# A mixture-of-experts layer behind two attentions: fewer expert tiles in two stages, rows fetched by token number and outputs written to token rows

## The reference

```
x = x + cross_attention(layernorm(x), ctx)       # 64 queries on 1601 keys, softmax
x = x + pairwise_attention(layernorm(x))         # relu(signed_sqrt(q_i + k_j)) for all pairs i, j of 64
x = x + experts(layernorm(x)):
    scores = sigmoid(xf @ gate.T)                # 8 experts, in 4 groups of 2; groups by scores + bias
    2 best groups, in them the 2 best experts; weights = their scores over their sum
    for e in range(8):                           # I = 256
        y += w[:, e] * ((silu(xf @ gate_proj[e].T) * (xf @ up_proj[e].T)) @ down_proj[e].T)
```

## Time and the profile before

| | |
|---|---|
| median of 3 runs | 634.35 us (634.19 to 635.99) |
| the profiled execution | 636.18 us, span 634.4 us, mean granted clock 0.954 |
| PE busy | 554.6 us (87%) |
| DVE busy | 421.3 us (66%) |
| ACT busy | 265.2 us (42%) |
| DMA | 196.3 MB, 309 GB/s over the span |

### The profile page before, as it was taken

One profiled execution on the slowest core, in us unless ns is written; L12 is line 12 of the kernel. 1 busy time (PEld: TensorE's weight loads), 2 busy tenths in 40 slices (PEclk: granted clock), 3 DMA queues, 4 the chain that ended last, 5 costly groups with the idle time before them and its releaser, 6 DMA issues.

```text
span 634.4 us, 7981 instructions
## 1 busy us (share of the span) xinstructions
PE 554.6 (87%) x2608; PEld 313.6 (49%) x2608; DVE 421.3 (66%) x721; ACT 265.2 (42%) x380; POOL 61.3 (10%) x76
## 2 busy tenths in 40 slices
PE   7899388999999999999999996669898989888960
PEld 3586133534445344453563442445666756655740
DVE  3775112568788687886978887785986865676623
ACT  0340021352623526235254182429666546465720
POOL 4000100100001000010000013000000610410004
PEclk9999777999999999999999999888999999999995
DMA  9999629979799797997959988634867899999916
GB/s 309 359 403 407 262 91 371 381 258 385 279 369 397 264 386 268 365 400 265 386 201 310 389 313 308 254 122 155 299 250 258 285 376 397 398 395 419 375 67 198
DMA packets 91677, 196.30 MB, mean 309 GB/s; under 512 B 5872, under 2 KB 39152, under 8 KB 87808
## 3 DMA queue, kind: packets, MB, share of 16 engines
q1 hardware_dynamic: 82400, 177.29, 75.9%
q10 hardware_dynamic: 6688, 10.25, 4.4%
q0 software_dynamic: 2560, 8.39, 3.7%
HBM read 173.89 MB, written 22.02 MB: 309 GB/s over the span
## 4 chain that ended last, share of the span: by engine, by line
PE 56%; DMA 15%; DVE 15%; ACT 5%; issue 4%; POOL 2%; SPq 2%; POOLq 0%; DVEq 0%; ACTq 0%
PE ps L1401 13%; PE ps L1491 11%; DMA gu_raw<-in_gu_t 6%; PE ps L1648 4%; DMA keys<-in_ctx_t 3%; DVE plane L925 2%; DVE wgu_lo L1167 2%; DMA rows<-in_x 2%; PE ps L1555 2%; PE ps L1618 2%; PE ps L1619 2%; DMA vals<-in_ctx 2%; PE ps L1626 2%; PE ps L314 2%; PE ps L315 2%
## 5 line engine op out<-in xcount | busy, mean ns | idle before, releaser
L1491 PE MATMUL ps<-vals,probs_t 128*64 128x512 f32 (+1 forms) x416 | 99.1, 616 | 2.2 <-DMA vals<-in_ctx 2.2
L1401 PE MATMUL ps<-keys,q_cur 128*64 128x401 f32 (+1 forms) x512 | 91.3, 509 | 8.6 <-DMA keys<-in_ctx_t 8.6
L1167 DVE TENSOR_TENSOR wgu_lo<-gu_raw,wgu_hi 128x2048 fp32r<-128x2048 f32 x30 | 68.6, 2288 | 37.8 <-ACT wgu_hi L688 37.8
L688 ACT CAST wgu_hi<-gu_raw 128x2048 fp32r<-128x2048 f32 x30 | 57.0, 1900 | 24.2 <-DMA gu_raw<-in_gu_t 24.2
L1401 PEld LDWEIGHTS ps<-keys,q_cur 128*64 128x64 f32 x512 | 35.5, 138 | 58.3 <-issue 49.0
L1648 PE MATMUL ps<-dn_raw,ht 128*128 128x512 f32 x120 | 58.4, 610 | 1.4 <-ACT ht L710 1.4
L1491 PEld LDWEIGHTS ps<-vals,probs_t 128*64 128x64 f32 (+1 forms) x416 | 28.1, 140 | 58.0 <-issue 57.7
L1618 PE MATMUL ps<-wgu_hi,xt_hi 128*128 128x512 f32 x120 | 50.8, 423 | 3.6 <-DVE xt_lo L1156 3.6
L1619 PE MATMUL ps<-wgu_hi,xt_lo 128*128 128x512 f32 x120 | 48.7, 406 | 0.0
L1005 DVE SCALAR_TENSOR_TENSOR plane<-plane,ps 128x512 f32<-128x512 f32 x64 | 40.3, 681 | 3.4 <-PE ps L1555 3.3
L517 POOL TENSOR_TENSOR x_in<-x_in,bv_b 128x512 f32<-128x512 f32 x8 | 10.1, 1267 | 276.8 <-DMA x_in<-in_x 276.8
(11 more groups left out here) (207 smaller groups left out, 939.7 us busy)
## 6 DMA issues: line engine op xcount, KB each, us to landing
keys<-in_ctx_t SPq DMA_DIRECT2D x24, 1604.0 KB, 12.9
gu_raw<-in_gu_t SPq DMA_DIRECT2D x30, 1024.0 KB, 7.5
vals<-in_ctx SPq DMA_DIRECT2D x32, 768.0 KB, 12.1
vals<-in_ctx SPq DMA_DIRECT2D x16, 1024.0 KB, 9.7
dn_raw<-in_down_t SPq DMA_DIRECT2D x30, 512.0 KB, 6.8
keys<-in_ctx_t SPq DMA_DIRECT2D x8, 1592.0 KB, 16.9
vals<-in_ctx SPq DMA_DIRECT2D x16, 512.0 KB
xs<-vy ACTq DMA_DIRECT2D x2, 3840.0 KB, 32.4
```

Of the source, the lines that this page charges most:

```text
L688: act.copy(wgu_hi[i % 2][:], gu_raw[i % 3][:]).then_inc(gu_hi_ok, 1)
L1167: dve.tensor_tensor(wgu_lo[i % 2][:], gu_raw[i % 3][:], wgu_hi[i % 2][:].bitcast(F32), ALU.subtract).then_inc(gu_lo_ok, 1)
L1401: ins = pe.matmul(ps[b * SQ:(b + 1) * SQ, c, 0:width(c)], q_cur[:, k, b * SQ:(b + 1) * SQ], keys[:, c, b * KD + k, 0:width(c)], start=(k = ...
L1491: ins = pe.matmul(ps[b * SQ:(b + 1) * SQ, OUT, :], probs_t[0:w, n, b * SQ:(b + 1) * SQ], vals[0:w, n % RING, b, :], start=(n == 0), stop=( ...
```

## The change

- One plan of 23 tiles (2*8+7). After token tiles 0 to 5 (`NA = 6`) only 5 tiles leave in the first stage, `FULL = 2*6-7`: those many are full whatever the data, since 1536 rows over 8 experts have at least 5 full tiles. Rows that are left over are placed again with those of token tiles 6 and 7, in the other 18. These start only when pair 7 has been gated and placed.
- The zeroing, `xs` and its scatters are gone. Normalised rows are stored in token order (`n3d`, direct DMAs). For each tile, the token number in each place is found by a product on PE of one-hot matrices (place within the tile by token) with a grid (token by tile, holding the token's number): `ids(g)`, `take_ids(g)`. POOL's `gather(i)` then fetches a tile's rows by number, and POOL's `scatter(i)` writes a tile's output straight to the token's row of `ys` (first or second choice); empty places write to spare rows behind them.
- So the final fetch is by direct DMAs: `load_first` (2 of 1 MB) when tile 21 is stored, `load_second` (8 of 256 KB) after the last.
- The 5 tiles of stage 1 use plain f32 products (`gate_up`, `copy_x`), the 18 others the split ones. `mask` is made in `pick` (4 more small links); `plan_full`, `keep_left`, `plan_rest`, `experts` are new.
- The order in pair 7 and behind it is new on each engine.

```diff
-    NA, NB = 4, 4
-    TILES = (2 * NA + 7, 2 * NB + 7)
-    NTILE = sum(TILES)
+    SETS = ((0, 4), (4, 6), (6, 8))
+    NA = 6
+    FULL = 2 * NA - 7
+    NTILE = 2 * NP + 7
...
             for c in range(NCH):
                 load_keys(NP - 1, c)
+            for t in range(4):
+                store_n3(t)
...
             sp.wait_ge(scored, NP * NCH)
...
+            sp.wait_ge(expert_ok, 1)
+            e = []
+            for i in range(3):
+                e.append(expert_of(i))
...
+            sp.wait_ge(expert_ok, 2)
+            for i in range(FULL, FULL + 3):
...
+            for i in range(FULL, NTILE):
                 if i + 3 < NTILE:
+                    e.append(expert_of(i + 3))
+                    load_gu(i + 3, e[i + 3])
                     load_dn(i + 3, e[i + 3])
...
+            stored(NTILE - 2)
+            load_first(0)
+            load_first(1)
+            stored(NTILE - 1)
+            for t in range(NP):
+                load_second(t)
...
+            def gather(i):
+
+                if i >= 4:
+                    pool.wait_ge(xt_tr, i - 3)
+                pool.indirect_dma_start(xg[i % 4][:], None, n3d[0:(NA if i < FULL else NP) * P, :],
+                                        bass.IndirectOffsetOnAxis(ap=token_i[:, i:i + 1], axis=0)).then_inc(xg_in[i % 4], 16)
+
+            def scatter(i):
+
+                pool.wait_ge(o_ok, i + 1)
+                pool.indirect_dma_start(ys, bass.IndirectOffsetOnAxis(ap=row_i[:, i:i + 1], axis=0), o_sb[i % 2][:], None
+                                        ).then_inc(o_out[i % 2], 16)
...
+            pool.wait_ge(ids_ok, 1)
+            pool.wait_ge(n3_out, 16 * NA)
+            for i in range(FULL):
+                gather(i)
+            for i in range(FULL):
+                scatter(i)
+            pool.wait_ge(ids_ok, 2)
+            pool.wait_ge(n3_out, 16 * NP)
+            for i in range(FULL, FULL + 4):
+                gather(i)
+            for i in range(FULL, NTILE):
+                scatter(i)
+                if i + 4 < NTILE:
+                    gather(i + 4)
...
-            act.wait_ge(zeros_ok, 1)
-            for g, n in enumerate(TILES):
-                act.dma_start(xs[g].rearrange("(n p) d -> p n d", p=P), vy[:, :].unsqueeze(1).to_broadcast([P, n, D])
-                              ).then_inc(zeros_out, 16)
...
+            high_gu(FULL)
+            high_gu(FULL + 1)
+            high_x(FULL)
```

```diff
             denominators(NP - 2)
-            low_gu(1)
-            stats3(NA, NP - 2)
-            weigh(0)
-            for i in range(NTILE):
+            low_norm_t(NP - 1)
+            copy_qk(NP - 1)
+            sum_half(NP - 1, 0)
+            relu_half(NP - 1, 0)
+            finish_pair(NP - 2)
+            stats3(6, 7)
+            sum_half(NP - 1, 1)
+            relu_half(NP - 1, 1)
+            keep_left()
+            gated(0)
...
+            gated(4)
+            take_logits(2)
+            pick(2)
+            plan_rest()
+            place_tokens(1)
+            experts(1)
+            take_ids(1)
+            low_gu(FULL)
+            low_x(FULL)
+            low_gu(FULL + 1)
+            for i in range(FULL, NTILE):
```

On PE, `both(7)` gains turn_x3(4), turn_x3(5) after attend(0), logits(4), logits(5) after attend(1) and count(0), and loses turn_x(0) ahead of project. Behind it:

```diff
+            ids(0)
+            norm_t(NP - 1)
+            pairwise_qk(NP - 1)
+            second_part(NP - 2)
+            values_y(NP - 1)
+            turn_x(0)
+            gate_up(0)
...
+            gate_up(4)
+            down(3)
+            turn_h(4)
+            turn_x3(7)
+            logits(6)
+            down(4)
+            logits(7)
+            count(1)
+            ids(1)
+            turn_x(FULL)
+            for i in range(FULL, NTILE):
                 gate_up_high(i)
                 if i + 1 < NTILE:
                     turn_x(i + 1)
                 gate_up_low(i)
```

More of the change, by code:

```diff
@@ L725, in both @@
                 if first_gate:
-                    for j in range(NA):
+                    for j in range(4):
                         copy_x3(j)
+                if last_pair(t):
+                    root3(4, 6)
                 if cross:
@@ L1240, in both @@
                 if last_pair(t):
-                    low_gu(0)
+                    experts(0)
+                    take_ids(0)
                 if pairwise:
@@ L1260, in _ @@
             denominators(NP - 2)
-            low_gu(1)
-            stats3(NA, NP - 2)
-            weigh(0)
-            for i in range(NTILE):
+            low_norm_t(NP - 1)
[8 more added lines that the diff above has]
+            gated(0)
+            inverse3(6, 7, 3)
+            apply3(6)
+            pairwise_softmax(NP - 1)
+            parts_of_ex(NP - 1)
+            gather_ex_t(NP - 1)
+            products(NP - 1, 0, 4)
+            gated(1)
+            products(NP - 1, 4, NC8)
+            sum_products(NP - 1, 0)
+            gated(2)
+            sum_products(NP - 1, 1)
+            place_sums(NP - 1)
+            denominators(NP - 1)
+            gated(3)
+            finish_pair(NP - 1)
+            stats3(7, 8)
+            inverse3(7, 8, 4)
+            apply3(7)
+            gated(4)
[9 more added lines that the diff above has]
+            for i in range(FULL, NTILE):
                 if i + 1 < NTILE:
@@ L1596, in count, with ids @@
                 ins.then_inc(count_mm, 1)
+            def ids(g):
+                T = (NA, NP)[g]
+                m = STAGE[g][1] - STAGE[g][0]
+                pe.wait_ge(one_hot_ok, g + 1)
+                pe.wait_ge(grid_ok, g + 1)
+                if g == 0:
+                    pe.wait_ge(logits_ok, 2)
+                else:
+                    pe.wait_ge(tmp_ok, NP)
+                grid = small["grid"][:, 0:2 * T * m].rearrange("p (n i) -> p n i", i=m)
+                for t in range(T):
+                    for w in range(2):
+                        ins = pe.matmul(ps[:, IDS_BANK[g], 0:m], one_hot[:, w, t, :], grid[:, w * T + t, :],
+                                        start=(t == 0 and w == 0), stop=(t == T - 1 and w == 1))
+                ins.then_inc(ids_mm, 1)
             def turn_x(i):
```

793 lines of the change are left out of this document (412 added, 381 removed).

## The result

The changed kernel takes 654.99 us (median of 6 runs, 648.08 to 656.07) against 635.0 us for the kernel before (6 runs, 632.13 to 636.58): a ratio of 1.0288, 95% interval 1.0229 to 1.0347. It is slower by 20 us, where 610 us with a range of 596 to 627 was predicted. The profiled execution took 648.64 us, its span is 646.8; the runs fall near 648 and near 656, and the trace is one of the lower ones, so what follows explains the traced execution and not the 6 us between it and the median.

The account below looks back on a forecast made before the run. It took the attention loop as PE-bound and untouched, and the tiles alone as filling PE and DMA. From the span, 634.4 - 14 - 9 - 1.5 + 0.5 = 610.4, so 610 us, range 596 to 627.

Parts of the forecast that it names:

- Step 4: The 17 periods of the last tiles: POOL's gather waits behind the scatter, period 5.9 us, 100.3 against 101.8, -1.5 us.
- POOL's round trip: Rival, tiles: slow indirect issues and longest landing give period 10.1, 681 us; decides from period 7.3; chance 0.04.
- It binds with the full landing: Rival, tiles: the POOL loop binds with landing 7.7, period 6.95, +18, 628 us; chance 0.12.
- Step 1: Head: zeroing writes go, the 8.60 us wait for keys goes and PE's clock stays up, -14 us.
- Step 2: Pair 7 up to its norm: added planning, transposes and ids(0) move the norm from 402.7 to 412.1, +9.4 us.
- Step 3: Pair 7's norm to the silu of the last 18 tiles' first: 412.1 to 499, -9 us against before.
- the bare chain costs more: Rival, stage 1 and planning: PE falls to 1.2 GHz and planning links cost 0.3, +10, 620 us; chance 0.13.
- Step 5: End, last silu to finish: faster loads paid for by eight more adds, 25.3 us against 24.7, +0.5 us.

Follow-up runs that it names:

- experiment 5: Changed kernel with the two 3.8 MB zero writes put back on ACT's queue, into a DRAM tensor nothing reads: 661.47 us.
- Experiment 1: Changed kernel with POOL issuing the gather of tile i+4 before the scatter of tile i: 613.03 us, ratio 0.9667.
- Experiment 2: Kernel before, with SP's direct load of a tile's rows one tile later, behind the store of the tile four ahead: 652.99 us, ratio 1.0261.
- experiment 3: Changed kernel with DVE's subtraction for the weights' low part in four 128x512 pieces in the last 18 tiles: 646.81 us, ratio 1.0183.
- Experiment 8: Changed kernel, gather first, stage 1 ids taken behind add_x of pair 7: 610.63 us; all parts together with 30 idle matmuls: 609.4 us.
- experiment 7: Changed kernel, gather first, 30 idle PE matmuls in stage 2's planning: 612.83 us; with all edits, 18 idle matmuls 604.62 us, none 608.16 us.
- Experiment 6: Changed kernel without planning of stage 2, its 18 tiles taking expert 0 and fixed rows: 631.75 us, ratio 0.9925.

## Why the prediction was wrong

By the steps of the forecast, on the profiled spans: 646.8 against 610.4, 36.4 us. The steps are read from one trace; the starts of pair 1's scores in experiment 5 show that a step read so can be some 2 us off.

**Step 4 failed, and with it the sign**: 126.1 us for 100.3, +25.8. The loop was named with its parts in the right order; two of three were mis-sized and one was drawn from a mean. For the round shown above, against the 11.8 us that a period of 5.9 stands for:
- turn_x to the end of the eviction: 4.75 forecast, 5.64 measured. The weights' low products ran slower behind most of the waits (L1776, four of them: 2.05 us behind the wait at 542.31, 1.55 to 2.06 behind six of the seven waits of tiles 9 to 21, 1.18 behind the one at 558.26; 1.17 in the tiles without one), and the granted clock was 0.73 between 541 and 545 us. The stall made its own loop longer.
- the end of the eviction to the gather's issue: 1.3 forecast, 2.62 measured. The scatter takes 2.04 us here and 1.49 to 2.43 in the others of the stretch, not 0.96.
- the gather to its use: 5.75 is what a period of 5.9 implies; 7.69 measured. I had 7.7 in hand and took "the middle" between a period of 6.9 and one that does not bind. The row under load already gave the full landing; the view over 510 to 610 us has 3.8/6.5/8.3 (least, median, most). Taken one by one from 505 us on, the gathers that PE waits for land in 6.1 to 8.3 us, the others in 3.8 to 6.5.

The sum is 4.15 us for two tiles. Over all 17 periods it is 3.04 for two, since the first and the last tiles don't wait: from the wait at 511.93 to the one at 606.09 two tiles take 15.7 us on average. Experiment 1 takes the loop away and gives back 33.9 us, more than the miss, since then the periods are at 5.39, below the 5.9. Experiment 2 shows that the same place makes PE wait with direct loads too, at a smaller loss; experiment 3 shows why the scatter's issue is long, but not what that costs.

Of the rivals, the one given 0.04 came true: "POOL's round trip", which was to decide from a period of 7.3 and a round trip of 9.9 us. Measured: 7.42 and 10.3. Its price of 681 was for a worse case than the one met. "It binds with the full landing" (period 6.95, 628 us, 0.12) had the landing right, 7.7 for the 7.69 measured; what it lacked were the long issue and the slower products. What was held against it, that nearly all indirect issues were 0.95 to 1.4 us, was counted over issues beside a quiet DVE; three of the eight scatters from 494 to 510 us took 2.19, 3.00 and 2.71 us, and each had a partner in the trace, which I did not look for. DVE's timeline of the kernel before has that of the second:

```profile
499.74 2.29 DVE L1167 TENSOR_TENSOR wgu_lo<-gu_raw,wgu_hi 128x2048 fp32r<-128x2048 f32 x1 [1.35 <-ACT wgu_hi L688]
```

It ends at 502.03, and the issue that began at 499.87 ends at 502.87. In the changed kernel each scatter is issued just behind the eviction, which is where DVE makes the next weights' low part: all 15 from 503 to 613 us are beside it.

**Step 1** was right in mechanism: 11.8 for 14.0. The wait went, but in this trace the clock did not stay up (0.83 from 70 to 90 us): the 40 and the 12 products of L1613 took 10.07 and 4.49 us for the forecast 8.9 and 2.7. In seven of the ten traces with this head the 12 took 2.80, so the 2.2 us that are missing are no more than one trace differs from another. The Trainium skill, "TensorE: Matmul & The Clock Gate", section "What's actually happening", has the array throttled by default and released by activity; by it the prediction put the gain at 10. The trace agrees with its direction, and the 11.8 lie between the two numbers.

**Step 2** was +11.5 for +9.4, right in kind: the eight products of L1613 ahead of the projection took 3.68 us (1.8 by the forecast's own rate of 6.23/28), with the clock at 0.67 from 380 to 400 us, and DVE waited 4.20 us for ids(0) with take_ids ahead of the reduction. Experiment 8 gives that order 2.1 us.

**Step 3**: tile 5's silu at 493.87, 505.7 on the clock of the trace before, for a forecast 499; of the 6.7 us, 2.1 are step 2's, the other 4.5 its own. Its count of DVE's links was good (logits to experts 12.8 forecast, 12.7 measured). What was undersized is PE's clock in a chain where PE stands still: 2 us were added for it, and the clock was 0.52 from 460 to 480 us. The trace of the changed kernel:

```profile
470.30 6.99 PE L1730 MATMUL ps<-grid,one_hot 128*128 128x18 f32 x32 [5.00 <-issue]
...
477.98 0.99 POOL L563 DMA_INDIRECT xg<-n3d,token_i  x1 [18.59 <-DVE token_i L1264]
...
484.95 1.13 PE L1744 MATMUL ps<-ident,xg 128*128 128x128 f32 x4 [7.67 <-DMA xg<-n3d,token_i]
```

ids(1) with take_ids was 3.1 in the sum and 6.7 here; experiment 7 brings ids(1) itself back from 6.98 to 3.72. The rival "the bare chain costs more" named this cause. The silus of tiles 4 and 5 are 41.2 us apart (33 to 37 were to show the step right). Experiment 6 prices the planning at 14 us, and the rest of the step's bare stretch is weights and rows in flight.

**Step 5**: 26.8 for 25.3 us. The first add is at 631.58, 11.6 behind the last silu (10.4 forecast), the rest as said.

In sum 2.2 + 2.1 + 4.5 + 25.8 + 1.5 = 36.1 of the 36.4; step 3's is counted from step 2's end, (493.87 - 402.44) less (499 - 412.1). The change's aim, fewer tiles, was met: the kernel with the order put right is 3.3% faster than before. What made it slower was one line's place in a queue.

## What to carry to other kernels

When a fetch moves to another queue, find what it now stands behind, and close the loop: from the instruction that starts the work to the one that waits for the fetched data, every leg at its loaded value, divided by the number of tiles in flight. A middle between "binds" and "doesn't" is neither: here it forecast 5.9 where 7.42 and 5.39 were the two answers. Issue loads ahead of stores in a shared queue, since the load has someone waiting. In a serial chain of small instructions, put the clock that the engine will have there into the sum, and try a little work without a use to hold it: 30 idle matmuls gave nothing here, 18 gave 3.5 us.

## What the runs showed of the hardware

- POOL's indirect DMA issue was held by DVE's subtraction of two SBUF operands: 0.97 us beside a quiet DVE, 1.49 to 2.43 beside the 2.29 us instruction. It ended 0.87 us behind it (547.10 + 2.29 = 549.39, 548.22 + 2.04 = 550.26), at 553.02 too (555.31 and 556.17), and 0.86 to 0.88 us behind it in all 15 scatters from 503 to 613 us. With four of 128x512 it was 1.43. The Trainium skill, "SBUF — State Buffer", section "SBUF: two separate sides", tells of descriptors that GpSimd cannot write while DVE runs an operation in a two-port mode, such as an f32 copy; an operation with two SBUF inputs it counts only against a GpSimd operation that reads SBUF. The trace agrees on the blocking and shows it for an f32 subtraction with two SBUF inputs; which port or operand blocks, no run shows.
- The Trainium skill, "DMA: Bandwidth & Descriptors", section "Anatomy of one DMA — SWDGE (gpsimd) path", would have 2.6 us for such a gather, an estimate by its figures. Measured in the tiles, with the DMA engines at 0.74: 3.8 at the least, 6.5 in the median, 7.7 in the round shown, 8.3 at the most; direct loads of the same size took 7.5 in the median in experiment 2, at 0.93. Here the indirect form was not the slower one from issue to landing.
- 32 small matmuls (128x18) took 6.99 us behind a PE that had stood still for most of 13 us, clock 0.52 from 460 to 480 us, and 3.64 behind one kept busy (experiment 7, clock 1.00 in the same stretch).
- With a wait that came back each second tile the granted clock of the whole stretch was 0.87, without it 1.00 (experiment 1), for the same matmuls.
